# Graph network layer stack: edge attribute sums taken chunk by chunk in storage order, and scatter records assembled as whole rows

## The reference

```python
# x: (6250, 64); edge_attr_64: (206250, 64); edge_attr_16: (206250, 16); edge_weight: (206250,)
# layer 0: two GIN convolutions: (x + segment_sum(x[src], dst)) @ W + b, relu between them
# layer 1:
messages = x[src] + x[dst] + edge_attr_64
out = segment_sum(messages, dst)
# layer 2, for each edge, summed by src:
edge_input = concat([x[row], x[col], edge_attr_16, edge_weight / 5.0])
h = silu(edge_input @ ew1 + eb1);  m_ij = silu(h @ ew2 + eb2)
agg = segment_sum(m_ij, row)           # then an MLP on concat([x, agg])
# layer 3:
msg = norm * (xc @ W1.T + b1 + xr * xc @ W2.T + b2)   # norm from the degrees, summed by row
```

## Time and profile before

| | us |
|---|---|
| median of three runs | 6490.53 |
| lowest, highest | 6486.48, 6493.28 |
| the profiled execution, its own time | 6465.67 |
| its span | 6464.0 |
| busy in the span: PE, DVE, POOL, ACT | 4506.1, 3365.5, 3893.9, 1498.8 |
| joint stage, first to last | 774.6 to 3547.9 |

### The profile page before, as it was taken

One profiled execution on the slowest core, in us unless ns is written; L12 is line 12 of the kernel. 1 busy time (PEld: TensorE's weight loads), 2 busy tenths in 40 slices (PEclk: granted clock), 3 DMA queues, 4 the chain that ended last, 5 costly groups with the idle time before them and its releaser, 6 DMA issues. The chain is left out here.

```text
span 6464.0 us, 125959 instructions
## 1 busy us (share of the span) xinstructions
PE 4506.1 (70%) x41113; PEld 3917.8 (61%) x41114; DVE 3365.5 (52%) x5567; ACT 1498.8 (23%) x2045; POOL 3893.9 (60%) x3580
## 2 busy tenths in 40 slices
PE   0000477766555535868694699999999999984995
PEld 0000266652222215858583599999999999973995
DVE  6898744457777741121310355555555555543333
ACT  0000000016666672000000122222222222221441
POOL 0000288888888887777877277777777777740000
PEclk9999699998888877969897699999999999986996
DMA  0400355543333348949794344444444444443882
GB/s 15 169 0 10 65 104 102 103 70 106 95 92 92 92 113 271 349 121 356 244 343 148 83 117 117 118 117 118 118 117 117 117 118 118 118 70 47 232 231 69
DMA packets 907314, 840.46 MB, mean 130 GB/s; under 512 B 326597, under 2 KB 816113, under 8 KB 903660
## 3 DMA queue, kind: packets, MB, share of 16 engines
q1 hardware_dynamic: 788028, 684.65, 34.6%
q0 software_dynamic: 119216, 154.89, 12.6%
HBM read 680.88 MB, written 156.42 MB: 130 GB/s over the span
## 5 line engine op out<-in xcount | busy, mean ns | idle before, releaser
L996 POOL DMA_INDIRECT out_records<-nodes_scatter_recs,nodes_scatter_rows x1650 | 1947.9, 1181 | 493.6 <-issue 493.6
L1738 POOL DMA_INDIRECT edge_mlp_b_rows<-b_table,edge_mlp_recs x1664 | 1583.7, 952 | 637.3 <-issue 414.5
L1241 PE MATMUL build_p_ring<-build_hot_near,build_hot_far 128*128 128x392 f16 x2400 | 553.2, 383 | 407.3 <-issue 224.5
L1241 PEld LDWEIGHTS build_p_ring<-build_hot_near,build_hot_far 128*128 128x128 bf16 x2400 | 255.0, 106 | 705.2 <-issue 608.5
L1792 PE MATMUL edge_mlp_p_pre<-edge_mlp_hot_t,edge_mlp_a_blk 128*128 128x128 f32 x3328 | 670.6, 283 | 8.5 <-DMA edge_mlp_b_rows<-b_table,edge_mlp_recs 6.6
L1793 PE MATMUL edge_mlp_p_pre<-c_ident,edge_mlp_b_rows 128*128 128x128 f32 x3328 | 646.1, 276 | 0.0
L1326 PE MATMUL sum_x_p_main<-sum_x_parts,sum_x_tiles 128*128 128x192 bf16 x5488 | 477.0, 251 | 226.5 <-DVE sum_x_parts L1269 178.9
L1852 DVE CAST edge_mlp_hot_t<-edge_mlp_p_turned 128x512 f32<-128x512 bf16 x416 | 287.8, 692 | 632.4 <-PE edge_mlp_p_turned L1784 632.4
L1326 PEld LDWEIGHTS sum_x_p_main<-sum_x_parts,sum_x_tiles 128*128 128x128 f16 x5488 | 466.2, 100 | 237.2 <-issue 187.2
L1127 PE MATMUL sums_p_sum<-sums_attr,sums_hot 128*128 x3328 | 450.4, 293 | 191.3 <-issue 172.0
L1761 PE MATMUL edge_mlp_p_m<-edge_mlp_w,edge_mlp_h 128*128 128x128 f32 x3328 | 576.2, 295 | 1.7 <-ACT edge_mlp_h L1819 1.7
(11 more groups left out here) (444 smaller groups left out, 6553.2 us busy)
## 6 DMA issues: line engine op xcount, KB each, us to landing
sum_x_tiles<-edge_counts SPq DMA_DIRECT2D x168, 768.0 KB
edge_mlp_a_blk<-a_table SPq DMA_DIRECT2D x1664, 64.0 KB
edge_counts<-build_plane SPq DMA_DIRECT2D x28, 3136.0 KB, 9.8
sum_z_tiles<-edge_counts SPq DMA_DIRECT2D x49, 1792.0 KB, 8.7
sum_y_tiles<-edge_counts SPq DMA_DIRECT2D x84, 768.0 KB
sums_attr<-in_edge_attr SPq DMA_DIRECT2D x100, 512.0 KB, 4.3
sum_x_tiles<-edge_counts SPq DMA_DIRECT2D x56, 832.0 KB
out_records<-place_padding SPq DMA_DIRECT2D x104, 256.0 KB, 2.1
```

Source lines behind the costliest of these rows:

```text
L996: pool.indirect_dma_start(out=out_rec, out_offset=bass.IndirectOffsetOnAxis(ap=rows[s][:, c:c + 1], axis=0), in_=recs[s][:, c], in_offset= ...
L1241: pe.matmul(p_ring[:, ds(banks[c], 1), 0:KEYS], hot_far[s][:, c // 2, :, c % 2], hot_near[s][:, c // 2, :, c % 2], start=False, stop=True, ...
L1738: pool.indirect_dma_start(out=b_rows[s][:, c], out_offset=None, in_=b_tab, in_offset=bass.IndirectOffsetOnAxis(ap=recs[s][:, c, FE + 1:FE ...
```

## The change

Items of `edge_sums`. The first 1612 items are the chunks in storage order, so item n lies in slot n mod 128 of `attr`, a constant in the code; `place_of_item` and its register loads go. The sum of such an item is that of the block of its first edge. Behind them, from item 1616 (`FIRST_MORE`), come 48 extra items, one for each block but the first: the chunk in which the block begins, once more, counted for that block alone (or for nothing, if the block begins with the chunk). SP loads these 48 chunks one by one, from rows that it reads from `more_row`, when three lanes have come free. A load may now overwrite a lane as soon as its own 16 items are through. `chunk_nodes` and the 13 gathers go; `near_of_item` comes from one subtraction on DVE for the chunks and from 13 matmuls with a selection matrix for the extras. The 19 gathers of L653 wait for these, since their target lies over the node numbers.

Scatter records. `place_out` assembles the whole record of 32 numbers: SP loads attributes in 11 pieces of 150 columns, ACT copies attributes, weight, `dst` and low bits into 125 x 150 records, SP stores them to a new DRAM tensor `records`, and the padding follows. `scatter_records` loads a piece with one DMA of whole rows, 128 partitions of 25 x 32 numbers, without a copy of meta numbers. `edge_meta` and three of four DVE operations of `tables_in` go.

```diff
@@ tables_in
-            step(dve.tensor_scalar(a.meta[0:EP, :, 0], a.weight[:], 1.0 / CUTOFF, None, ALU.mult))
-            step(dve.tensor_copy(a.meta[0:EP, :, 1].bitcast(I32), a.ends["in"][:]))
-            step(dve.tensor_scalar(a.ints[:], a.ends["out"][:], P - 1, None, ALU.bitwise_and))
-            step(dve.tensor_copy(a.meta[0:EP, :, 2], a.ints[:]))
+            step(dve.tensor_scalar(a.low[:], a.ends["out"][:], P - 1, None, ALU.bitwise_and))
@@ plan_windows, gpsimd
-            pool.wait_ge(b_made, 1)
-            pool.wait_ge(nodes_in, 16)
-            for i in range(IB):
-                pool.indirect_dma_start(
-                    out=b_got[:, i], out_offset=None, in_=chunk_nodes,
-                    in_offset=bass.IndirectOffsetOnAxis(ap=b_chunk[:, i:i + 1], axis=0)).then_inc(b_gathered[i * SLOTS // IB], 16)
             pool.wait_ge(chunk_made, 1)
             pool.wait_ge(stored, 16)
+            pool.wait_ge(b_turned, 1)
+            pool.wait_ge(moved_made, 1)
             for i in range(IT):
@@ plan_windows, tensor
             pe.wait_ge(b_asked, 1)
-            pe.transpose(p_b_turn[0:IB, 0], bf[0][:], k["ident"][:])
-            pe.transpose(p_b_turn[0:IB, 1], bf[3][:], k["ident"][:]).then_inc(b_turned, 1)
+            pe.transpose(p_b_turn[0:IB, 0], bf[2][:], k["ident"][:])
+            pe.wait_ge(sel_made, 1)
+            pe.wait_ge(keys_cut, 2)
+            for q in range(IB):
+                mm = pe.matmul(p_b_turn[:, 1, 0:NB - 1], nodes[:, q], b_sel[:, q], start=q == 0, stop=q == IB - 1)
+            mm.then_inc(b_turned, 1)
@@ place_out, sync
+            def assemble(source16):
+                attrs = source16.rearrange("(p c) w -> p c w", p=EP)
+
+                def load(j):
+                    if j >= 2:
+                        sp.wait_ge(made[j % 2], 4 * (j // 2))
+                    sp.dma_start(attr[j % 2][:], attrs[:, j * WIDE:(j + 1) * WIDE]).then_inc(attr_in[j % 2], 16)
+
+                load(0)
+                for j in range(pieces):
+                    if j + 1 < pieces:
+                        load(j + 1)
+                    sp.wait_ge(made[j % 2], 4 * (j // 2 + 1))
+                    sp.dma_start(lines[0:EP, j * WIDE:(j + 1) * WIDE], recs[j % 2][:]).then_inc(stored[j % 2], 16)
@@ place_out, scalar and gpsimd
+            act.wait_ge(cleared, 2)
+            for j in range(pieces):
+                s, at = j % 2, slice(j * WIDE, (j + 1) * WIDE)
+                if j >= 2:
+                    act.wait_ge(stored[s], 16 * (j // 2))
+                act.mul(recs[s][:, :, FE], a.weight[:, at], 1.0 / CUTOFF).then_inc(made[s], 1)
+                act.copy(recs[s][:, :, FE + 1].bitcast(I32), a.ends["in"][:, at]).then_inc(made[s], 1)
+                act.copy(recs[s][:, :, FE + 2], a.low[:, at]).then_inc(made[s], 1)
+                act.wait_ge(attr_in[s], 16 * (j // 2 + 1))
+                act.copy(recs[s][:, :, 0:FE], attr[s][:]).then_inc(made[s], 1)
+            for s in range(2):
+                nc.gpsimd.memset(recs[s][:], 0.0).then_inc(cleared, 1)
@@ scatter_records
-                pool.dma_start(recs[s][0:EP, :, 0:FE], recs_of[:, at]).then_inc(rec_in[s], 16)
-                nc.gpsimd.tensor_copy(recs[s][0:EP, :, FE:FE + 3], meta[0:EP, at]).then_inc(staged[s], 1)
-                nc.gpsimd.tensor_copy(rows[s][:], row[:, at]).then_inc(staged[s], 1)
+            pool.dma_start(recs[s][:], lines[:, at]).then_inc(rec_in[s], 16)
+            nc.gpsimd.tensor_copy(rows[s][:], row[:, at]).then_inc(staged[s], 1)
@@ edge_sums, sync
-                            sp.wait_ge(summed, i * (LANES * per_load) + (u * per_load - (LANES - 1 - SPREAD) * per_load))
+                            sp.wait_ge(summed, i * (LANES * per_load) + ((u + 1 - LANES) * per_load))
+                for e in range(0, NB - 1, BATCH):
+                    sp.wait_ge(summed, (rounds - 1) * (LANES * per_load) - MORE * per_load + (e // LOADED + 1) * per_load)
+                    _, rows = nc.values_load_multi_w_load_instructions(
+                        k["more_row"][0:1, e:e + BATCH], engines=[SP], min_val=0, max_val=E - P,
+                        skip_runtime_bounds_check_because="where a chunk of edges begins")
+                    for c in range(min(BATCH, NB - 1 - e)):
+                        sp.dma_start(attr[:, (LANES - MORE) * LOADED + e + c, 0:F], source64[ds(rows[c], P)]).then_inc(more_in, 16)
@@ edge_sums, tensor
+                    if isinstance(i, int) and i == rounds - 1 and u == LANES - MORE:
+                        pe.wait_ge(more_in, 16 * (NB - 1))
-                        _, places = nc.values_load_multi_w_load_instructions(
-                            k["place_of_item"][0:1, at], engines=[PE], min_val=0, max_val=LANES * LOADED - 1,
-                            skip_runtime_bounds_check_because="the low bits of a chunk's number")
-                                           attr[:, ds(places[c], 1)].rearrange("p o f -> p (o f)"), start=False, stop=True,
-                                           skip_group_check=True)
+                                           attr[:, lo + n * BATCH + c], start=False, stop=True, skip_group_check=True)
```

More of the change, by code:

```diff
@@ L548, in plan_windows @@
         keys, nodes = sb("keys", [P, EDGE_TILES, 2, P]), far.bitcast(F32)
[L549 to L554, removed]
+        b_near = part[:].bitcast(F32)
+        b_first, b_same, b_base = sb("b_first", [P, NB - 1]), sb("b_same", [P, NB - 1]), sb("b_base", [P, NB - 1])
+        b_no, b_sel = sb("b_no", [P, IB]), sb("b_sel", [P, IB, NB - 1])
+        bf, bi = [sb(f"bf{n}", [P, IB]) for n in range(3)], sb("bi", [P, IB], I32)
+        turned_b = sb("turned_b", [IB, P], I32)
         final = sb("final", [P, P])
@@ new lines, in stage, with send @@
+        def stage(i, s, done):
+            at = ds(i * (3 * SC) + s * SC, SC)
+            wait_count(pool, scattered[s], done * (16 * SC))
+            turnstile(pool, k["gate"], s, passed)
+            pool.dma_start(recs[s][:], lines[:, at]).then_inc(rec_in[s], 16)
+            nc.gpsimd.tensor_copy(rows[s][:], row[:, at]).then_inc(staged[s], 1)
+        def send(i, s):
+            pool.wait_ge(rec_in[s], i * 16 + 16)
+            pool.wait_ge(staged[s], i + 1)
+            turnstile(pool, k["gate"], s, passed)
+            for c in range(SC):
+                pool.indirect_dma_start(
+                    out=out_rec, out_offset=bass.IndirectOffsetOnAxis(ap=rows[s][:, c:c + 1], axis=0),
+                    in_=recs[s][:, c], in_offset=None).then_inc(scattered[s], 16)
@@ L1010, in scatter @@
+        rounds = PIECES // 3
+        stage(0, 0, 0)
+        for i in steps(pool, rounds - 1):
             stage(i, 1, i)
@@ L1013, in scatter @@
             send(i, 1)
+            stage(i + 1, 0, i + 1)
             send(i, 2)
-        flag = nc.values_load(k["unsorted"][0:1, 0:1], engines=[POOL], min_val=0, max_val=E,
-                              skip_runtime_bounds_check_because="a count of edges")
-        with pool.If(flag > 0):
-            scatter(in_rec[:, F + 2:F + 2 + FE])
-        with pool.Else():
-            scatter(ea16)
+        i = rounds - 1
+        stage(i, 1, i)
+        send(i, 0)
+        stage(i, 2, i)
+        send(i, 1)
+        send(i, 2)
         for s in range(3):
@@ L2026, in gnn_stack @@
         k = alloc_constants(nc, ctx)
-        for name in ("scatter", "edge_mlp", "plan", "blocks"):
+        for name in ("scatter", "edge_mlp", "plan"):
             k["dma_" + name] = [ctx.enter_context(nc.semaphore(f"dma_{name}{s}")) for s in range(SLOTS)]
@@ L2064, in gnn_stack @@
                 together = Together(nc, nodes_ctx)
[L2065 to L2066 removed]
+                scatter_records(nc, k, together, recs, recs_rows, row, lin_rec, out_rec, (rec_in, staged, passed, scattered))
                 edge_sums(nc, together, k, ea64, in_rec, ea_sums)
```

175 lines of the change are left out of this document (79 added, 96 removed).

## The result

The changed kernel takes 6385.1 us (median of four runs, 6383.1 to 6394.0), the kernel before 6491.9 us beside it (6486.5 to 6499.7): a ratio of 0.984, 95% interval 0.982 to 0.985. The profiled executions stand closer together, 6394.0 against 6465.7 us, since that of after is the slowest of its four (8.9 us over the median) and that of before was faster than all of its own.

A forecast was written before the change was run, and what follows sets the result against it. POOL's scatter was taken to bound the joint stage; +10.4 us before it and -218 on POOL gave -208, so 6490.5 became 6283 us (6256 in the profiled span), range 6225 to 6365.

The forecast's parts named there:

- What bounds the kernel: Joint stage: POOL's `scatter_records` ends it last; DVE waits 77.7 us, so savings on other engines are worth nothing.
- Before the stage: Stages before the joint one: `tables_in` -3.9, `plan_windows` +12.3, `place_out` +2 with assembly hidden; +10.4 us in all.
- The plain DMA: Scatter, joint stage: POOL's issue per piece falls from 3.84 to 0.95 us, saving 185 us (0 to 225).
- the first rival: Scatter: issuing a plain DMA on POOL costs the same whatever its rows, giving 6468 us; chance 0.08.
- The copy of meta: Scatter, joint stage: the 0.46 us copy (L988) goes from 64 pieces, saving 29 us.
- The start: Joint stage: stage start to first scatter DMA falls from 32.3 to 8 us, saving 24 us (13 to 26).
- Contention: Scatter in the build: without the old plain DMA's shelter, DVE's work stretches more indirect DMAs, +20 us (0 to +30).
- The other chain: `edge_sums`: ends at 3363, about 3240 with stall relief, saving 125 us in register loads; against POOL's end, worth 0.
- Rival 2: Joint stage: the chain of the sums becomes the bound; 6305 without stall relief, 6431 without any gain; chance 0.12.
- Rivals 1 and 3: 1: the first rival. 3: assembly in `place_out` overruns, making the kernel slower, 6533 us; chance 0.03.
- rival 4: Plan wait and late first load cost double, scatter contention grows; about 6330 us, inside the range, no chance of its own.
- What follows is untouched: From `message_out`, forecast to start at 3340, to the end: the 2916 us stay as they were.

The follow-up runs named there:

- held pairs: Kernel before, changed kernel and each half alone, compared with one register operation ahead of each build wait on a loaded count: 6509.2, 6428.2, 6308.5 (records), 6611.0 us (sums).
- before_held: Kernel before plus one register operation ahead of each build wait that goes by a loaded count: 6509.2 us.
- records_only: Against before_held: only assembled records, whole-row scatter DMA and no meta copies added; sums and plan as before: 6308.5 us.
- build_split_b: Against after_held: the build's 128x3136 comparison on VectorE made in four operations of 128x784: 6102.5 us.
- edge_split_b: Against after_held: in `edge_mlp` the 128x512 comparison made in four operations and the cast in two: 6378.3 us.
- all_three: Against after_held: the edits of psum_operand_b, edge_split_b and build_split_b together: 6067.3 us, ratio 0.935 to the kernel before.
- after_held: Changed kernel plus one register operation ahead of each build wait that goes by a loaded count: 6428.2 us.
- two_lists_b: Against after_held: TensorE again fetches a list of places per batch of the sums, slowing them to about the old pace: 6377.4 us.
- psum_operand_b: Against after_held: the row of numbers the sums' comparison reads lies in PSUM instead of SBUF: 6321.6 us.
- sums_only: Against after_held: new sums and plan kept, but the old scatter with 64-byte rows and meta copies: 6611.0 us.

## Why the prediction missed

- *What bounds the kernel*: right. POOL ends the joint stage in both kernels, DVE waits for it.
- *Before the stage*: right. +11.3 for +10.4 (786.1 against 774.8); the keys' first gather at 748.5 for 749.3; `place_out` hid the assembly: 25.1 us from store to store, 276 us in eleven for the 300 of the sum, and the padding issued by 545 for 576.
- *The plain DMA*: right in mechanism, low in size: 0.58 us and not 0.95, so 64 x 3.26 = 209 us for 185. The issue time went with the number of rows: 3125 rows 3.84 us, 128 rows 0.58. The Trainium skill's "DMA: Bandwidth & Descriptors", "Anatomy of one DMA — SWDGE (gpsimd) path", on which the first rival leaned, says that many descriptors can be emitted before the added cost shows. The trace doesn't bear it out here: 2997 rows more cost 3.26 us. The copy of meta gave its 29, but the copy that stays grew from 355 to 542 ns, 12 back: 26 of the 66 now begin inside a tensor_tensor of DVE, 8 before. The start: 5.0 us behind the stage's start for 8, 27 saved for 24.
- *Contention*: the step that failed. I took 20 us, from "the same DVE work meets L996", and only in the build; the busy time of the scatter grew by 2040.6 - 1947.9 = 93: 49 in the sums, 37 in the build and 7 behind them. By the held pairs the records half accounts for 38 of the growth (what the 20 were for) and the faster sums for 54, for which the sum had no term. How much is lost depends on how many DMAs begin inside an operation, and that depends on the period of DVE against POOL's 1.26 us. I read this pace only for PE's chain, to price it at nothing.
- *The other chain, "worth 0"*: its end moved as forecast or better (3075 for 3240, since all stalls went). But the sums half, priced at nothing but its plan, is worth less than that: with the new records in place it costs the joint stage 67 us, 12 of them the plan, and the kernel 120, the rest of them in `edge_mlp`. Rival 2 asked whether that chain gets too late; nobody asked what it does to POOL when it gets faster. Rivals 1 and 3 did not come up; rival 4 had the right word, contention, at less than half of what was missing (6330, 47 us over the forecast, for 102).
- *"What follows is untouched"*: the code was, the time was not: 2984.6 us for 2916.1, 62 of the 68 more in `edge_mlp`. That DVE's operations stretch its gathers is shown; why more of them begin inside the comparison in this kernel is open.

The sum of the profile: forecast 6256, measured 6392.3. Of the 136 us, 68 are in the joint stage (3407.7 for 3340) and 68 behind it. Two errors partly cancel, which was luck: the plain DMA saved 24 us more than forecast, and contention cost 73 more. The records half alone was forecast well: its terms sum to -220 with tables and place, and the held pair measured -201 (-221 in the profiled executions).

## What to carry to other kernels

An engine that is off the critical path still acts on the one that is on it. When a change speeds it up, look up what its operations do to the other's while they run, count how many of the other's instructions fit between two of them before and after, and price that; slack does not make them free. Where POOL issues indirect DMAs beside DVE, keep DVE's comparisons of two SBUF operands short, or move one operand to PSUM: splitting one comparison in four was worth more here than the whole change.

## What the hardware did that I had not expected

- An indirect DMA on POOL that begins during a DVE tensor_tensor with both operands in SBUF ends 0.83 us behind the end of that operation, whatever was left of it; with one operand in PSUM it takes its plain 0.96 us, 1.01 at most. DVE's own times don't change (1.23 us in both).
- A copy on POOL is stretched as well, to 0.06 us behind the operation (24 of 28); a plain DMA issued by POOL is not (0.60 us at most, 18 of 28 begun inside one). A cast on DVE stretched the gathers in `edge_mlp` (128x512 f32 to bf16, 195 of 199), while the casts of 128x3136 in the passes, also from SBUF to SBUF, did not: 20 scatter DMAs begin during them in after and none takes over 1.01. What tells the casts apart was not looked into.
- Four comparisons of 128x784 take 4 x 0.50 us in line, the one of 128x3136 takes 1.79, and the build is no longer for it.
- `edge_mlp` has two paces for the same code: 2099 to 2106 us in six of these profiles (before, before_held, records_only, build_split_b, edge_split_b, all_three) and 2154 to 2166 in five (after, after_held, two_lists_b, psum_operand_b, sums_only). Two of the six have its operations split. Of the rest, what chooses the pace was not found: all five have the new sums and their plan, but so has build_split_b, which takes 2104. That it is gathers which begin inside the comparison is shown; why they fall so is open.
- A register operation ahead of each of the build's 448 waits on ACT and 600 on PE lengthened it by 58 us; which of the two did it was not told apart.
